# Output projection of batch b moved into the K/V phase of batch b+1, with doubled row buffers and unrolled programs, in a float32 adaLN attention and MoE block

## What is computed

```python
h = layernorm(x) * (1 + ca) + sa            # ca, sa, ga, ...: rows of silu(c) @ wmod, one per batch
Q, K, V = split(layernorm(h)*gamma+beta @ W_in + b_in)
K, V = rotary(K), rotary(V)
A = 0.5 * sum_rows(K/|K| * V/|V|) + 0.5     # one factor per feature, over all 512 rows of the batch
x = x + ga * ((A * Q) @ W_out + b_out + h)
h = layernorm(x) * (1 + cb) + sb
x = x + gb * (relu(h @ W_up.T) @ W_down.T + sum(softmax(top2(h @ W_gate.T))) * (h @ W_expert))
```

## Time and profile before

| | |
|---|---|
| median of 3 runs | 401.91 us (400.4 to 402.61) |
| the profiled execution, own time | 401.95 us |
| its span, first to last instruction | 400.2 us |
| instructions | 5269 |
| PE busy | 375.3 us, 94% |
| PEld, DVE, ACT, POOL busy | 73%, 66%, 43%, 28% |
| mean granted PE clock | 0.960 |
| transfers | 27.32 MB, mean 68 GB/s |

### The profile page before, as it was taken

One profiled execution on the slowest core, in us unless ns is written; L12 is line 12 of the kernel. 1 busy time (PEld: TensorE's weight loads), 2 busy tenths in 40 slices (PEclk: granted clock), 3 DMA queues, 4 the chain that ended last, 5 costly groups with the idle time before them and its releaser, 6 DMA issues.

```text
span 400.2 us, 5269 instructions
## 1 busy us (share of the span) xinstructions
PE 375.3 (94%) x1664; PEld 292.3 (73%) x1664; DVE 263.8 (66%) x513; ACT 173.6 (43%) x309; POOL 112.0 (28%) x108
## 2 busy tenths in 40 slices
PE   4997999599996999996999999999999999999996
PEld 0155888488884888875888877778778878887886
DVE  0767779863899717999269995962852556074454
ACT  1236486165553645744541559235313611371220
POOL 0115046510668104683027543840001000100000
PEclk9968799799999699998999999999999999999999
DMA  7985972010000230000000003020200020011002
GB/s 223 401 330 191 366 255 112 0 52 0 2 0 0 35 123 0 0 0 0 0 2 0 2 0 105 15 92 0 80 26 0 26 79 0 0 40 65 1 2 106
DMA packets 10944, 27.32 MB, mean 68 GB/s; under 512 B 1184, under 2 KB 1568, under 8 KB 9776
## 3 DMA queue, kind: packets, MB, share of 16 engines
q1 hardware_dynamic: 10928, 27.13, 19.4%
HBM read 22.90 MB, written 4.23 MB: 68 GB/s over the span
## 4 chain that ended last, share of the span: by engine, by line
PE 61%; DVE 13%; issue 4%; ACT 3%; DVEq 0%; ACTq 0%
PE ps L981 19%; PE ps L982 18%; PE ps L983 18%; PE ps L1005 3%; DVE acc L698 1%; DVE prod L680 1%; DVE prod L687 1%; DVE ps L668 1%; DVE tmp L734 1%; DVE kv L670 1%; PE ps L1105 1%; PE ps L1106 1%; DVE prod L685 1%; DVE pair L709 1%; DVE fold L706 1%
## 5 line engine op out<-in xcount | busy, mean ns | idle before, releaser
L981 PE MATMUL ps<-w_hi,t_hi 128*128 128x512 f32 x192 | 75.9, 395 | 0.0
L983 PE MATMUL ps<-w_hi,t_lo 128*128 128x512 f32 x192 | 75.5, 393 | 0.0
L982 PE MATMUL ps<-w_lo,t_hi 128*128 128x512 f32 x192 | 75.4, 393 | 0.0
L661 DVE TENSOR_TENSOR t_lo<-ps,t_hi 128x512 fp32r<-128x512 f32 x32 | 22.0, 690 | 58.7 <-ACT t_hi L468 58.7
L981 PE MATMUL ps<-t_hi,w_hi 128*128 128x512 f32 x128 | 53.6, 419 | 0.0
L982 PE MATMUL ps<-t_lo,w_hi 128*128 128x512 f32 x128 | 52.1, 407 | 0.0
L983 PE MATMUL ps<-t_hi,w_lo 128*128 128x512 f32 x128 | 51.8, 405 | 0.0
L981 PE MATMUL ps<-w_hi,g_hi 128*128 128x512 f32 (+1 forms) x132 | 51.5, 390 | 0.0
L983 PE MATMUL ps<-w_hi,g_lo 128*128 128x512 f32 (+1 forms) x132 | 50.7, 384 | 0.0
L982 PE MATMUL ps<-w_lo,g_hi 128*128 128x512 f32 (+1 forms) x132 | 50.5, 383 | 0.0
L314 POOL TENSOR_TENSOR hrs<-hve,expo 128x2 f32<-128x2 f32 (+1 forms) x12 | 10.7, 892 | 117.4 <-DVE hve L652 97.5
(11 more groups left out here) (130 smaller groups left out, 634.4 us busy)
## 6 DMA issues: line engine op xcount, KB each, us to landing
xs<-in_X SPq DMA_DIRECT2D x4, 1024.0 KB, 7.4
stage<-in_w SPq DMA_DIRECT2D x4, 1024.0 KB, 7.6
out<-xs SPq DMA_DIRECT2D x15, 256.0 KB, 2.0
xs<-in_wmod SPq DMA_DIRECT2D x3, 1024.0 KB, 10.3
xs<-in_wmod SPq DMA_DIRECT2D x8, 256.0 KB, 6.9
stage<-in_w SPq DMA_DIRECT2D x8, 256.0 KB, 9.5
gate_bc<-mod_rows SPq DMA_DIRECT2D x8, 256.0 KB, 5.2
gate_bc<-in_wmod SPq DMA_DIRECT2D x1, 1024.0 KB, 12.3
```

The source lines that it names most:

```text
L661: v.tensor_tensor(t_lo[:, c, :], ps[:, T_BANKS[c % 2], :], t_hi[:, c, :].bitcast(f32), ALU.subtract).then_inc(t_los, 1)
L981: mm(dst, l_hi, r_hi, start=start, stop=False)
L982: mm(dst, l_hi, r_lo, start=False, stop=False)
L983: return mm(dst, l_lo, r_hi, start=False, stop=stop)
```

## The change

It keeps `t_hi`, `t_lo` and the rows of h in two copies (`[g % 2]`), drops `tmp` (bias and output are added in place in `hb`), and reorders the programs of all engines. On PE, the four projection tiles of batch b (`out_rows_of(b)`) stand behind the first K/V tile of batch b+1; those of batch 3 stand in `ffn(0)` behind the router and two expert tiles. `a_sums` comes after the fourth Q chunk and after all transposes, and uses bank 6. All loops are written out, and waits are on constants. The diff, cut to what sets the order:

```diff
@@ PE @@
-            def attention(b, last):
+            def attention(b):
+                kv_tile(b, 0)
+                if b > 0:
+                    out_rows_of(b - 1)
+                for t in range(1, NT):
                     kv_tile(b, t)
                 for c in range(NC):
...
-                    feature_chunk(Q_BANKS[c], WQ, c, q_ps, (lambda: a_sums(b)) if c == 2 else None)
-                for c in range(NC):
-                    pe.wait_ge(q_los, b * NC + c + 1)
...
+                    feature_chunk(b, Q_BANKS[c], WQ, c, q_ps)
+                    if c == (2 if b == 0 else 1):
                         transposes(b + 1, 0)
                         transposes(b + 1, 1)
+                    if c == (3 if b == 0 else 2):
                         transposes(b + 1, 2)
                         transposes(b + 1, 3)
+                a_sums(b)
...
             def a_sums(b):
                 pe.wait_ge(afold, b * 3 + 3)
+                pe.wait_ge(t_los, (b + 1) * NC + 3)
@@ PE, ffn @@
                 done.then_inc(lg_ps, 1)
+                if b == 0:
+                    expert_rows(0, 0)
+                    expert_rows(0, 1)
+                    out_rows_of(B - 1)
@@ ACT @@
+            def attention(b):
+                if b > 0:
+                    for c in range(NC):
+                        q_evac(b - 1, c)
+                if b == 0:
+                    x_sums(1)
+                norm_sums(b, 0)
+                if b == 0:
+                    x_squares(1)
+                    normalise_x(1)
+                elif b + 2 < B:
+                    x_sums(b + 2)
+                    x_squares(b + 2)
+                norm_sums(b, 1)
+                if b == 0:
+                    split_hi(3)
+                elif b < B - 1:
+                    normalise(b + 1, 0, 2)
+                norm_sums(b, 2)
+                if b == 0:
+                    normalise(1, 0, 2)
+                elif b < B - 1:
+                    normalise(b + 1, 2, 2)
+                else:
+                    normalise(B, 0, NT)
+                norm_sums(b, 3)
+                if b == 0:
+                    normalise(1, 2, 2)
+                if b == B - 1:
+                    split_hi(5)
+                t_evac(b + 1, 0)
+                t_evac(b + 1, 1)
+                if b == 0:
+                    x_sums(2)
+                    x_squares(2)
+                t_evac(b + 1, 2)
+                t_evac(b + 1, 3)
+                if b + 2 < B:
+                    normalise_x(b + 2)
...
+            split_hi(4)
+            for c in range(NC):
+                q_evac(B - 1, c)
+            split_hi(6)
+            for b in range(B):
+                ffn(b)
@@ DVE @@
+            def finish_rows(b):
+                o_evac(b, 0)
+                o_evac(b, 1)
+                x2_out(b, 0)
+                o_evac(b, 2)
+                x2_out(b, 1)
+                o_evac(b, 3)
+            def attention(b):
+                if b > 0:
+                    a_evac(b - 1)
+                    for c in range(NC):
+                        q_split(b - 1, c)
+                if b == 0:
+                    x_mean(1)
+                kv_rows(b, 0)
+                kv_products(b, 0)
+                if b > 0:
+                    finish_rows(b - 1)
...
+                else:
+                    x_var(1)
+                kv_sum(b, 0)
+                if b == 0:
+                    x_shift(1)
+                elif b < B - 1:
+                    h_row(b + 1, 0)
+                    h_row(b + 1, 1)
+                    h_stats(b + 1, 0)
+                    h_stats(b + 1, 1)
+                    h_aggr(b + 1, 0, 2)
...
+                kv_rows(b, 1)
...
+                kv_products(b, 1)
+                if 0 < b < B - 1:
+                    h_shift(b + 1, 0, 2)
+                    h_row(b + 1, 2)
...
+                elif b == 0:
+                    h_row(1, 0)
+                    h_row(1, 1)
...
+                kv_sum(b, 1)
+                kv_rows(b, 2)
...
+                kv_products(b, 2)
...
+                kv_sum(b, 2)
+                kv_rows(b, 3)
+                kv_products(b, 3)
+                if b == 0:
+                    h_shift(1, 2, 2)
+                kv_sum(b, 3)
+                a_pairs(b)
+                t_split(b + 1, 0)
+                t_split(b + 1, 1)
+                if b == 0:
+                    for k in range(NC):
+                        split_lo_out(k)
+                    x_mean(2)
+                t_split(b + 1, 2)
+                t_split(b + 1, 3)
+                if b == 0:
+                    x_var(2)
+                    x_shift(2)
@@ POOL @@
             def scale_rows(g, t):
                 pool.wait_ge(xn_s, g * NT + t + 1)
-                pool.wait_ge(base_s, (g - 1) * NT + t + 1)
+                if g >= 2:
+                    pool.wait_ge(x2_dve if t < 2 else x2_pool, (g - 2) * 2 + t % 2 + 1)
+            def attention(b):
+                weight(b, 0)
+                if b == 0:
...
+                else:
+                    if b < B - 1:
+                        scale_rows(b + 1, 0)
+                        scale_rows(b + 1, 1)
+                    x2_out(b - 1, 2)
+                    x2_out(b - 1, 3)
+                    if b < B - 1:
+                        scale_rows(b + 1, 2)
+                        scale_rows(b + 1, 3)
+                    weight(b, 1)
+                    if b + 2 < B:
+                        rstd_x(b + 2)
+                    if b < B - 1:
+                        rstd_h(b + 1, 0, 2)
+                        weight(b, 2)
+                        rstd_h(b + 1, 2, 2)
...
+                pool.wait_ge(afold, b * 3 + 3)
...
+                    for t in range(NT):
+                        base(b + 1, t)
@@ SP @@
+            load_x(1)
+            sp.wait_ge(row_out, 32)
+            load_modulation(1)
             sp.wait_ge(gate_out, 32)
             for b in range(B):
                 sp.dma_start(gate_bc[:, b * D:(b + 1) * D], ...)
-            load_x(1)
```

More of the change, by code:

```diff
@@ L353, in attention @@
-            def attention(b, last):
-                first = isinstance(b, int) and b == 0
-                if not first:
+                nc.gpsimd.tensor_tensor(h_row_of(g, t), z[:, t, :], ca_bc[:], ALU.mult).then_inc(scaled_s, 1)
+            def attention(b):
+                weight(b, 0)
+                if b == 0:
+                    rstd_x(1)
+                    scale_rows(1, 0)
+                    scale_rows(1, 1)
+                    weight(b, 1)
+                    scale_rows(1, 2)
+                    scale_rows(1, 3)
+                    weight(b, 2)
+                    rstd_h(1, 0, 2)
+                    weight(b, 3)
+                    rstd_h(1, 2, 2)
+                    rstd_x(2)
+                else:
+                    if b < B - 1:
+                        scale_rows(b + 1, 0)
+                        scale_rows(b + 1, 1)
@@ L396, in _ @@
             low_part(6, whi, (5,) * NC, wlo_down)
-            with pool.Fori(0, B - 1) as b:
-                rstd_h(b + B + 1, 0, NT)
+            for g in range(B + 1, 2 * B):
+                rstd_h(g, 0, NT)
         @block.scalar
@@ L542, in _, with ffn @@
                 split_hi_k(c)
[L543 removed]
+                t_evac(0, c)
             split_hi(2)
             act.wait_ge(mod_sb, 6)
[L546 to L552 removed]
+            for b in range(B):
+                attention(b)
+            def ffn(b):
+                last = b == B - 1
                 act.wait_ge(lg_ps, b + 1)
[L554 removed]
+                nc.scalar.activation(lgt, ps[0:2 * NE, SMALL_BANK, :], ACT.Copy).then_inc(lg_t, 1)
                 for c in range(NC):
@@ L969, in ffn @@
                         d_evac_last(i)
-            with dve.Fori(0, B - 1) as b:
-                ffn(b, False)
-            ffn(B - 1, True)
+            a_evac(B - 1)
+            for c in range(NC):
+                q_split(B - 1, c)
+            split_lo(4)
+            finish_rows(B - 1)
+            for b in range(B):
+                ffn(b)
         @block.tensor
@@ L1084, in _ @@
                 pe.wait_ge(mod_sb, i + 1)
-                mm(ps[:, 2 + i, :], ones[:], rows[0:1, i, :], start=True, stop=True).then_inc(bc_ps, 1)
+                mm(ps[:, 2 + i, :], ones, rows[0:1, i, :], start=True, stop=True).then_inc(bc_ps, 1)
             mod_row(4, x_slot(1), wm_in[2:3])
@@ L1150, in ffn @@
                         transposes(b + B + 1, 3)
-            with pe.Fori(0, B - 1) as b:
-                ffn(b, False)
-            ffn(B - 1, True)
+            for b in range(B):
+                ffn(b)
 def layout(inputs):
```

511 lines of the change are left out of this document (215 added, 296 removed).

## The result

The changed kernel takes **405.78 us** (median of 6 runs, 404.22 to 406.29) against 401.66 us (6 runs) for the kernel before on the same chip: ratio **1.0096** [1.0068, 1.0125], slower by some 4 us. Its profiled execution took 405.63 us with a span of 403.9, so its trace stands for the median.

The account below looks back on a forecast made before the run. PE was taken as busy nearly all the time, waiting three times about 4 us for the pair tile. Terms: 22.6 gained - 19.5 - 3.0 - 1.5 = -1.4, span 401.6, time 403.3 us; range 394.5 to 409.

Parts of the forecast that it names:

- forecast case: Whole kernel: the summed forecast of 403.3 us holds, own range some 398 to 407; chance 0.5.
- no change: Whole kernel: within about 0.5% (2.0 us) of before, 399.9 to 403.9; chance 0.28.
- Batch 0: First batch: 19.5 us of waits, with PE stops near 58 us (2), 74 us (6) and 85 us (6).
- `h_row` beside POOL: DVE row operations in batch 0: 1.8 us each beside POOL's row scaling instead of 0.7 alone; 2.3 us open.
- Batch 1 +3.0, batch 2 +1.5, batch 3 0: PE waits for the next batch's rows and first low part, POOL being tight: 3.0, 1.5 and 0 us.
- ffn(0) 0: Feed-forward start: later W_down load and moved projection cost nothing, unless the load is 3 us late.
- Unrolling 0: Written-out loops: more instruction packets, not slower matmuls; 0 taken, ends -1 and +2 us.
- DVE and POOL don't collide: Faster rival: 396.5 us, middle 398, if `h_shift` in batch 1 waits less than 0.5 us; chance 0.30.
- The clock: Slower rival: stops in batches 1 and 2 bring PE to 1.2 GHz, 407 to 409 us; chance 0.15.
- above about 2 us: Sign for the clock rival: a PE stop in batches 1 and 2 longer than about 2 us decides it.
- the gain is not touched by batch 0: Rival: the two 6 us stops in batch 0 don't exist, x(2)'s statistics hidden: 391 us; chance 0.05.

Follow-up runs that it names:

- experiment 4: Changed kernel with x(2)'s statistics moved into idle times of ACT and normalise_x(2) behind q_evac(0): 404.62 us, ratio 1.0113 to the kernel before.
- experiment 5: experiment 4 plus one line: POOL's base rows of batch 0 wait until DVE has made W_out's four low parts: 397.29 us, ratio 0.9929 to the kernel before.
- experiment 1: Kernel before the change with every hardware loop written out and nothing else changed: 399.74 us, ratio 0.9979.
- experiment 2: Changed kernel with x(2)'s statistics behind all four transposed chunks instead of between chunks 1 and 2: 409.95 us, ratio 1.0246 to the kernel before.
- experiment 6: experiment 3 plus POOL's base rows of batch 0 held until W_out's four low parts are made: 399.00 us, ratio 0.9950 to the kernel before.
- experiment 3: Changed kernel with x(2)'s statistics moved into idle times of ACT, normalise_x(2) still ahead of q_evac(0): 404.66 us, ratio 1.0108 to the kernel before.
- experiment 7: Changed kernel with the squares of K/V tile 1 ahead of normalise_x(1) on ACT: 403.57 us, ratio 1.0088 to the kernel before.
- experiment 10: Changed kernel with one expert tile instead of two ahead of the last projection in ffn(0): 403.96 us, ratio 1.0064 to the kernel before.

## Why the prediction came out as it did

I forecast 403.3 us, range 394.5 to 409, and slower by over 0.5% at 0.38, the largest of the three chances. The time is 2.5 us above, on the slow side of the forecast case's own range (398 to 407), so the sum was right in kind and a little short. Part of the nearness is luck. The forecast time itself, 0.4% above before, lay within what I had called no change; "slower" led "faster" by 0.38 to 0.34 only; and in batch 0 a miss was offset by the opening. Term by term, in spans (401.6 forecast, 403.9 measured):

- **Batch 0**, the 19.5 us that eat the gain: right in kind, 1.8 us short. Counting back 24 + 48 matmuls from 113.48, batch 1 starts in effect at 97.2 (forecast 96.6). But batch 0 began at 38.75 instead of 39.96, as the opening was shorter in this execution, which no term had foreseen; so its waits are 21.3 us. `x_sums(1)` began 8.5 us behind x(1)'s issue (7.1 put down), the chain from there to the transposes took 35.0 us (35.8), and from the transposes to batch 1's start in effect it was 17.5 us (16.3), of which 1.1 is `x_shift(2)` beside POOL's base rows, a collision I had not put down. The first stop was 3.1 us rather than 2.1, since PE wanted the bank 1.6 us sooner than I had it (1.2 of it by the opening) while the release came within 0.5 us of the forecast; the second was 2.9 instead of 6.2, as PE came to it later by the slow matmuls of the first; transposes at 79.63 (80.3), third stop to 92.1 (some 6 us, yes).
- **`h_row` beside POOL**, 1.8 us each: held, with the delay shared out otherwise. In batch 0 two took 2.37 us and the accumulation behind them 2.02 instead of 1.02, 2.1 us of delay in all where I counted 2.3; in batch 1 two took 3.47. By the Trainium skill (SBUF — State Buffer, Who interferes with whom) a DVE operation with two SBUF inputs and a GpSimd operation that reads SBUF exclude each other; these rows agree, and so do experiments 4 and 5: 6.58 us for four such operations beside POOL's rows, 2.49 without.
- **Batch 1 +3.0, batch 2 +1.5, batch 3 0**: measured +3.5, +1.7, -0.1 against 46.4 (batch 1 from 97.2). `h_shift` waited 1.78 us for POOL (forecast 2.5), and `t_split` behind `a_pairs` held PE for 1.9 and 1.5 us (forecast 1.6 and 0.2).
- **ffn(0) 0**: wrong, +0.9 us (49.58 against 37.78 + 10.88 before). This is the step that I left out. I checked W_down's load, which cost nothing, and not what moving the expert tiles ahead of the projection takes from the transposes behind them: half of the matmuls that covered `normalise`.

```profile
275.20 2.93 ACT L480 ACTIVATE z<-xs,hnm,hrs 128x512 f32<-128x512 f32 x4 [3.33 <-DVE hnm L684]
...
278.24 1.06 PE L1064 MATMUL ps<-idn,z 128*128 128x128 f32 x8 [1.56 <-issue]
```

- **Unrolling 0**: held (experiment 1).

Sum of the misses: 0.6 (1.8 less 1.2 of the opening) + 0.5 + 0.2 - 0.1 + 0.9 + 0.1 (the later ffn) = 2.2 of the 2.3 us.

Of the rivals, "DVE and POOL don't collide" fell by its own sign: `h_shift` in batch 1 waited 1.78 us, not less than 0.5. "The clock" did not decide in the changed kernel: PE stopped 1.9 us in batch 1 (142.40) and the granted clock stayed at 1.00. But the mechanism exists at just that stop. In experiment 4 the same 1.9 us stop was followed by 1.2 GHz (PEclk is the column behind POOL); first experiment 4, then the changed kernel, from 140 to 146 us:

```profile
140.00:146.00 6.00, 5.96 (x26) 4.91 (x26) 1.96 (x3) 5.21 (x8) 4.44 (x4) 0.72 0.00 0
```

```profile
140.00:146.00 6.00, 4.08 (x22) 3.04 (x21) 3.78 (x8) 3.70 (x7) 4.18 (x4) 1.00 0.00 0
```

There the last Q chunk took 4.3 instead of 2.8 us. So the length of a stop alone, as in my "above about 2 us", does not decide: with this stop at 1.9 us in all eight kernels that have it, the clock fell in experiments 2, 4 and 6, and not in 3, 5, 7 or 10 or the changed kernel. The Trainium skill (TensorE: Matmul & The Clock Gate, The HAM clock gate) has the gate watch PE's recent activity with a phase that varies from run to run, which is compatible with this; no run here shows the phase.

How far "the gain is not touched by batch 0" (391) is from what can be had, the runs show: 397.3 with x(2)'s statistics hidden and the base rows held (experiment 5), and 393.6 only with the cures in batches 1 and 2 and in ffn(0) as well.

## What to carry to other kernels

When work is moved off the end of a stage, ask what it covered for the *first* pass, whose inputs are not prefetched: here a change that saves three waits of 4 us lost more in batch 0 alone. A stop's length says little; find the chain that ends it and measure that chain (35.0 us in nine kernels), because taking away a stop inside the chain's shadow (4.7 us on PE in experiment 7) gives little (0.8). And when a delay is removed, look at what it held back: POOL's base rows, freed early, took from DVE most of what ACT had gained, until one wait put them behind DVE's two-input operations.

## What the runs showed of the hardware that I had not expected

DVE's small and one-input operations were delayed beside POOL too: `acc<-prod,wgt` (a TENSOR_SCALAR of 128x768 in SBUF) took 0.62 us at 53.42, with no row operation on POOL, and 1.73 us at 114.48, as POOL went from one row to the next; `ab_col` (128x4) took 1.13 us at 95.74 beside a base row. Batch normalisation statistics (one SBUF input, 0.64 us each) kept their time beside POOL at 119.52:

```profile
53.42 0.62 DVE L724 TENSOR_SCALAR acc<-prod,wgt 128x768 f32<-128x768 f32 x1
...
95.74 1.13 DVE L745 TENSOR_TENSOR ab_col<-a_col,col 128x4 f32<-128x4 f32 x1
...
114.48 1.73 DVE L724 TENSOR_SCALAR acc<-prod,wgt 128x768 f32<-128x768 f32 x1
...
119.52 1.27 DVE L667 BATCH_NORM_STATS2 hst<-hb 128x6 f32<-128x512 f32 x2
...
114.49 1.29 POOL L347 TENSOR_TENSOR hb<-hb,gate_bc 128x512 f32<-128x512 f32 x1
```

And the opening of one and the same code, from the start to W_q's issue, took between 28.2 and 32.3 us in twelve profiled executions. The times of the kernel before spread over 5.8 us on one chip (397.29 to 403.05), so the opening may be a good part of that; this is not shown, and what moves the opening is open too.
